# A one-core transformer layer whose opening is reordered: loads queued by need, stacks copied on chip

## The chip, the cores and the metric

The kernel runs on one core of a Trainium2 chip. The metric is the device time of one execution in microseconds; several runs are made and the median is taken. The core has five engines with a queue of instructions each: TensorE (PE, matmuls into PSUM), VectorE (DVE), ScalarE (ACT), GpSimd (POOL) and SyncE (SP, which here only issues transfers). They wait for each other through semaphores that are written out by hand.

## The reference

A pre-norm layer on x of shape (4, 256, 256): four batches of 256 rows of width 256. All of it is in float32.

```
h = layernorm(x)
q, k, v = h @ Wq.T, h @ Wk.T, h @ Wv.T
q, k = q*cos + rotate_half(q)*sin, k*cos + rotate_half(k)*sin     # over the whole width of 256
split into 16 heads of 16
mem_out = elu1(q) @ (elu1(k).T @ v) / (elu1(q) . sum elu1(k))     # elu1(t) = elu(t) + 1
attn = softmax(q @ k.T / 4) @ v
x = x + (sigmoid(gate)*mem_out + (1 - sigmoid(gate))*attn) @ Wo.T
h = layernorm(x)
x = x + fwht(silu(h @ W1.T) * (h @ W3.T)) @ W2.T                  # hidden width 1024
```

fwht is the normalised Walsh-Hadamard transform along the hidden axis. The kernel applies it to W2 instead of to the hidden values, once, at the start.

## The kernel before, in words

**Precision.** Each float32 operand of the projections is split into a high part (rounded by a ScalarE copy to float32r) and a low part (the rest, by a subtraction). A product is three matmuls: high by high, high by low, low by high.

**The stacks.** For the scores, the split sits in the contraction instead. `q_stack` and `k_stack` hold for each of 16 heads a column block of 256 and, on the partitions, three slots of 16 rows: q is (high, low, high), k is (high, high, low), so that one matmul sums the three products. Rows 48 to 63 are zero. Rows 64 and 65 are one in `k_stack`; in `q_stack` they are zero in the score pass and hold the negated row maximum (high, low) in the exp pass, so that the second product comes out shifted. `rotate_half` pairs column i with i + 128, so q and k are computed turned, with features on the partitions: a tile for the first 128 (c = 0) and one for the second (c = 1), and heads 0 to 7 lie in the first, 8 to 15 in the second. The rotated values (`roped`) are split into `part_hi` and `part_lo`, written to DRAM (`parts`, L261) and read back into the slots with the head moved from the partitions to the columns (`load_stacks`, L263 to L275), six copies of 128 KB for each half of the heads.

**The rounds.** The batches go through a pipeline of rounds, from -1 to 4. In round r the attention of batch r and the feed-forward part of batch r - 1 are computed, and q, k, v of batch r + 1 are prepared. A round has a score phase (`scores`, then the row maxima on VectorE, L628), the transpose of the maxima (L911), two small transfers of the negated maxima into row 64 and 65, and an exp phase (`shifted_scores` L919, exp on ScalarE L367, the product with v L936). The stacks of batch r + 1 are loaded in round r, half by half, as soon as the exp phase has read eight heads (L269). All of the order is written out by hand, engine by engine; each engine works through its list in order, and SP's list of transfers is one more such queue.

**The opening** (round -1). SP loads x0, Wq, Wk, x1, W1, W3; when the splits of Wq, Wk, Wv are done, W2 (it shares their buffer `narrow_raw`), then x2, x3, and four pieces of Wo. ACT's queue loads the gate, the constants and Wv. GpSimd zeroes both stacks (L490, L534), sets ones in rows 64 and 65 (L536), and subtracts for the low parts of W1 and W3 (L542). ScalarE splits Wq, Wk, Wv (L313), copies the turned rows (L319), and splits W1 and W3 (L411). VectorE does the layer norm of batch 0 (L592 to L611), the low parts of the weights (L762), the rotation (L639, L644), the low parts of q and k (L649), the negative part (L653) and the features (L660). TensorE: transpose, q and k, v, transpose of batch 1, `hadamard(0)`, features turned (L948), `hadamard(1)`, scores of heads 0 and 1, memory (L959). Then round 0 begins with the projections of batch 1 mixed into the score phase, and `hadamard(2)` and `hadamard(3)` at heads 6 and 7.

**W2.** Four hadamard products (L1046, 128 rows of the transform each) and three butterflies, the first on GpSimd, the others on VectorE (L233), all in place between `w2_raw` (the same memory as Wq, Wk, Wv raw) and `w2_b` (that of W3 raw). So W2 can be loaded only after the splits of Wq, Wk and Wv, and the first butterfly waits for the low part of W3 (L227).

## Time and profile before

| | us |
|---|---|
| median of 3 runs | 251.93 |
| lowest, highest | 249.94, 252.10 |
| profiled execution | 254.45 |
| its span, first to last instruction | 252.6 |
| TensorE matmuls busy | 200.2 (79%) |
| VectorE busy | 174.9 (69%) |
| ScalarE busy | 97.8 (39%) |
| GpSimd busy | 95.7 (38%) |

The span is that of the profiled execution; its own time is 1.85 us longer than the span. The mean granted clock of TensorE is 0.932 of full speed. In the first 50 us TensorE is idle for more than half of the time.

### The profile page before, as it was taken

The page shows a single profiled execution, that of the slowest core. Times are in us where ns is not written, and L with a number is a line of the kernel's source. Part 1 is how long each engine was busy: PE and PEld are TensorE (multiplying, and loading weights), DVE is VectorE, ACT ScalarE, POOL GpSimd, SP SyncE. Part 2 cuts the span into 40 slices and gives each one's busy share as a digit, 9 for nine tenths or more (in the row PEclk, how much of TensorE's full clock was granted, in tenths as well). Part 3 has the DMA queues.
Part 4 walks back from the last instruction along what each step waited for, and adds up shares of the span by engine and source line. Part 5 has one row for each costly group of instructions (what it writes and reads, how often), then busy time and mean ns, then how long its engine had stood idle before and what let it go on. Part 6 is the DMA issues. An engine that isn't in the chain of part 4 may idle for free.

```text
span 252.6 us, 4048 instructions
## 1 busy us (share of the span) xinstructions
PE 200.2 (79%) x1444; PEld 169.1 (67%) x1444; DVE 174.9 (69%) x341; ACT 97.8 (39%) x196; POOL 95.7 (38%) x73
## 2 busy tenths in 40 slices
PE   0064066886897949999999699999879999959894
PEld 0064055873544939997788599877769986748893
DVE  6966862498898597838879967448998562962442
ACT  2261131042884012368810325686021577312231
POOL 7919500069450738323610492152021215111332
PEclk9999655799997997999999899999999999997999
DMA  6919299313087103002790130066800100000101
GB/s 217 384 29 260 86 176 120 38 43 130 0 122 114 22 31 111 31 2 51 79 128 1 43 114 20 4 91 99 109 0 0 49 0 3 1 1 0 44 0 42
DMA packets 16940, 17.67 MB, mean 70 GB/s; under 512 B 1676, under 2 KB 16268, under 8 KB 16908
## 3 DMA queue, kind: packets, MB, share of 16 engines
q1 hardware_dynamic: 16168, 16.68, 31.9%
q10 hardware_dynamic: 752, 0.73, 0.9%
q8 instruction: 11, 0.18, 0.4%
q14 instruction: 9, 0.07, 0.1%
HBM read 11.93 MB, written 5.24 MB: 68 GB/s over the span
## 4 chain that ended last, share of the span: by engine, by line
PE 43%; issue 22%; DVE 17%; POOL 8%; DMA 6%; SPq 2%; ACT 2%; POOLq 0%; DVEq 0%; ACTq 0%
DVE rowmax_pad L628 5%; DMA k_stack<-parts 5%; PE score_bank L901 5%; PE score_bank L1010 4%; PE exp_bank L919 4%; DVE xn L611 4%; PE down_bank L1032 4%; POOL hid_lo L525 4%; PE exp_bank L1010 3%; PE misc_bank L848 2%; DVE prod L639 2%; PE pv_bank L936 2%; PE misc_bank L849 2%; PE misc_bank L850 2%; PE misc_bank L969 2%
## 5 line engine op out<-in xcount | busy, mean ns | idle before, releaser
L628 DVE TENSOR_REDUCE rowmax_pad<-score_bank 128x2 f32<-128x512 f32 x64 | 42.8, 685 | 17.8 <-PE score_bank L901 17.8
L525 POOL TENSOR_TENSOR hid_lo<-wide_raw,hid_hi 128x256 fp32r<-128x256 f32 x32 | 25.0, 782 | 70.6 <-ACT hid_hi L400 67.1
L367 ACT ACTIVATE prob<-exp_bank 128x512 f32<-128x512 f32 x64 | 37.8, 601 | 15.4 <-PE exp_bank L919 15.1
L901 PE MATMUL score_bank<-k_stack,q_stack 128*128 128x256 f32 x128 | 31.1, 337 | 14.7 <-DVE rowmax_pad L628 10.5
L901 PEld LDWEIGHTS score_bank<-k_stack,q_stack 128*128 128x128 f32 x128 | 21.8, 205 | 20.0 <-DVE rowmax_pad L628 10.8
L919 PE MATMUL exp_bank<-q_stack,k_stack 128*128 128x256 f32 x128 | 28.5, 306 | 2.5 <-DMA q_stack<-nmT_lo 1.4
L919 PEld LDWEIGHTS exp_bank<-q_stack,k_stack 128*128 128x128 f32 x128 | 19.2, 189 | 14.0 <-issue 8.2
L506 POOL TENSOR_TENSOR roped<-prod 128x512 f32<-128x512 f32 x6 | 7.6, 1271 | 44.0 <-DVE prod L639 44.0
L738 DVE SCALAR_TENSOR_TENSOR wide_raw<-wide_raw,score_bank 128x256 f32<-128x256 f32 x16 | 6.7, 418 | 23.3 <-ACT wide_raw L394 23.3
L861 PE MATMUL misc_bank<-cst,xn 128*128 128x128 f32 x16 | 3.4, 351 | 23.9 <-DVE xn L611 23.9
L1032 PE MATMUL down_bank<-w_hi,hid_hi 128*128 128x256 f32 x64 | 17.5, 296 | 1.4 <-ACT hid_hi L400 1.4
L861 PEld LDWEIGHTS misc_bank<-cst,xn 128*128 128x128 f32 x16 | 2.3, 178 | 24.1 <-issue 13.1
L988 PE MATMUL pv_bank<-wo,att 128*128 128x256 f32 x64 | 16.3, 382 | 1.7 <-DVE att L723 1.7
L611 DVE TENSOR_SCALAR xn<-xs,mv,rstd 128x256 f32<-128x256 f32 x16 | 12.3, 809 | 7.6 <-POOL rstd L499 7.3
L1010 PE MATMUL exp_bank<-h2T_hi,w_hi 128*128 128x256 f32 x64 | 17.4, 294 | 0.0
L1010 PE MATMUL exp_bank<-h2T_hi,w_lo 128*128 128x256 f32 x64 | 17.1, 288 | 0.0
L1010 PE MATMUL score_bank<-h2T_hi,w_hi 128*128 128x256 f32 x64 | 17.0, 289 | 0.0
L1032 PE MATMUL down_bank<-w_lo,hid_hi 128*128 128x256 f32 x64 | 16.5, 281 | 0.0
L1010 PE MATMUL score_bank<-h2T_hi,w_lo 128*128 128x256 f32 x64 | 16.4, 280 | 0.0
L379 ACT ACTIVATE xs<-pv_bank 128x512 f32<-128x512 f32 x4 | 2.4, 598 | 35.1 <-DVE stats L592 35.1
L325 ACT ACTIVATE part_hi<-roped 128x512 fp32r<-128x512 f32 x8 | 5.0, 630 | 27.8 <-POOL roped L506 20.3
L936 PE MATMUL pv_bank<-prob,v_strips 128*32 128x256 f32 x192 | 15.3, 391 | 0.1
(117 smaller groups left out, 547.4 us busy)
## 6 DMA issues: line engine op xcount, KB each, us to landing
q_stack<-parts SPq DMA_DIRECT2D x24, 128.0 KB
k_stack<-parts SPq DMA_DIRECT2D x24, 128.0 KB
parts<-part_hi SPq DMA_DIRECT2D x8, 256.0 KB, 2.2
parts<-part_lo SPq DMA_DIRECT2D x8, 256.0 KB, 2.4
xs<-in_x SPq DMA_DIRECT2D x4, 256.0 KB, 6.6
wide_raw<-in_w1T SPq DMA_DIRECT2D x1, 1024.0 KB, 8.2
wide_raw<-in_w3T SPq DMA_DIRECT2D x1, 1024.0 KB, 10.0
narrow_raw<-in_w2T SPq DMA_DIRECT2D x1, 1024.0 KB, 6.0
```

The lines of the kernel that those rows point to most:

```text
L367: act.activation(prob[:, h % 8], exp_bank[h % 2][:], ACT.Exp, scale=SCALE).then_inc(prob_s, 1)
L506: pool.tensor_tensor(roped[:, c], prod[:, 2 * c], prod[:, 2 * c + 1], (ALU.subtract, ALU.add)[c]).then_inc(rope_sum, 1)
L525: pool.tensor_tensor(hid_lo[:, n % 3, :], ffn_work[n % 3], hid_hi[:, n % 3, :].bitcast(F32), ALU.subtract).then_inc(hid_lo_s, 1)
L611: dve.tensor_scalar(xn[:, tt, :], xs[:, b, tt, :], mv[:, tt, 0:1], rstd[:, tt:tt + 1], ALU.subtract, ALU.mult).then_inc(ln_xn, 1)
L628: dve.tensor_reduce(rowmax[:, h, :], score_bank[h % 2][:], AX.X, ALU.max).then_inc(rowmax_s, 1)
L738: dve.scalar_tensor_tensor(out=work, in0=work, scalar=1.0, in1=chunk_bank(n)[:, 0, :], op0=ALU.add, op1=ALU.mult).then_inc(gated_s, 1)
L901: mm = pe.matmul(bank[:, tt, :], q_stack[:, h, tt * P:tt * P + P], k_stack[:, h, :], start=True, stop=True)
L919: mm = pe.matmul(bank[:, tt, :], k_stack[:, h, tt * P:tt * P + P], q_stack[:, h, :], start=True, stop=True)
L936: mm = pe.matmul(bank[STRIP * j:STRIP * j + STRIP, half, :], v_strips[b % 2][:, tt, h, :], prob[:, h % 8, tt, :], start=(tt == 0), stop=(t ...
L988: mm = pe.matmul(bank[:, tt, :], att[:, g, tt * P:tt * P + P], wo[:, g, :], start=False, stop=(g == NG - 1), skip_group_check=True)
L1010: pe.matmul(bank[:, m, :], w[:, m, k, cols], h2T_hi[:, k, :], start=(k == 0 and w is w13_hi), stop=False)
L1032: pe.matmul(bank[:, tt, :], hid_hi[:, n % 3, tt * P:tt * P + P], w[:, c, :], start=(c == 0 and tt == 0 and w is w2_hi), stop=False, skip_g ...
```

## The change

**SP's queue.** After x0, Wq, Wk, x1, W1 it issues three transfers that fill rows 48 to 65 of `q_stack` with zeros, rows 48 to 63 of `k_stack` with zeros and rows 64 and 65 of it with ones, from a small tile `fill` of two times 256 columns that GpSimd sets. Then come the twelve stack copies of batch 0 and only then W3, W2, x2, the four pieces of Wo, x3.

**The stacks.** The columns of Wq and Wk and the rows of the tables are put in another order outside of the timed kernel (`by_dim`), so that partition p of a part holds dimension p // 8 of head p % 8. A copy then goes from `part_hi` or `part_lo` on chip straight to a slot; `parts` in DRAM, its writes and its semaphores go. The four copies of the high part are issued when that is ready, the two of the low part when that is. Splits of a later batch wait for these copies (`stack_in`) instead of for the writes. The matmuls read rows 0 to 65 of the stacks instead of all 128.

**GpSimd.** The memsets of the stacks go. W1's low part comes in four pieces ahead of round 0, W3's in four pieces in round 0, between the low parts of batch 1 and the first butterfly.

**ScalarE.** It splits W1 after `exp_elu(0)` and W3 after the copy of the turned features, instead of both ahead of v. All four hadamard products are copied out in round 0, between the two high parts of batch 1.

**VectorE.** `low_hT(0)` comes after the low part of Wk instead of before it, `ln_normalise(1)` ahead of the rope products.

**TensorE.** All four hadamard products come in round 0's score phase, after heads 5, 6, 7 and 8.

```diff
-            for m, w in enumerate((w1T, w3T)):
-                sp.dma_start(wide_raw[:, m], w.rearrange("(c p) n -> p c n", p=P)).then_inc(w13_in[m], 16)
-            sp.wait_ge(wqkv_hi_s, 3)
...
+            sp.dma_start(wide_raw[:, 0], w1T.rearrange("(c p) n -> p c n", p=P)).then_inc(w13_in[0], 16)
+            sp.wait_ge(fill_set, 2)
+            for rows, value in ((q_stack[3 * HD:MAXROW + 2], 0), (k_stack[3 * HD:MAXROW], 0), (k_stack[MAXROW:MAXROW + 2], 1)):
+                n = rows.shape[0]
+                sp.dma_start(rows.bitcast(F32), fill[0:n, value, :].unsqueeze(1).broadcast_to([n, NH, S])).then_inc(stack_zero, 16)
+
+            def late_loads():
+                sp.dma_start(wide_raw[:, 1], w3T.rearrange("(c p) n -> p c n", p=P)).then_inc(w13_in[1], 16)
+                sp.wait_ge(wqkv_hi_s, 3)
+                sp.wait_ge(wqkv_lo_s, 3)
+                sp.dma_start(w2_raw, w2T.rearrange("(c p) n -> p c n", p=P)).then_inc(w2_in, 16)
+                sp.dma_start(xs[:, 2], xv(x, 2)).then_inc(x_in[2], 16)
+                sp.wait_ge(wo_zero, 1)
...
+                sp.dma_start(xs[:, 3], xv(x, 3)).then_inc(x_in[3], 16)
...
             def load_stacks(b, c):
-                sp.wait_ge(parts_out[c], 32 * (b + 1))
                 if b == 0:
-                    sp.wait_ge(stack_zero, 2)
+                    sp.wait_ge(stack_zero, 48)
                 else:
                     sp.wait_ge(exp_ps, NH * (b - 1) + HH * (c + 1))
                     sp.dma_start(q_stack[MAXROW:MAXROW + 2, HH * c:HH * c + HH, :].bitcast(F32),
-                                 k_stack[MAXROW + 2:MAXROW + 4, HH * c:HH * c + HH, :].bitcast(F32)).then_inc(stack_in[c], 16)
-                for m, stack, slots in ((0, q_stack, (0, 1, 0)), (1, k_stack, (0, 0, 1))):
-                    for s, half in enumerate(slots):
-                        sp.dma_start(stack[HD * s:HD * s + HD, HH * c:HH * c + HH, :].bitcast(F32),
-                                     parts[b, half, c, m].rearrange("(h d) n -> d h n", d=HD)).then_inc(stack_in[c], 16)
+                                 fill[0:2, 0, :].unsqueeze(1).broadcast_to([2, HH, S])).then_inc(stack_in[c], 16)
+                for src, ready, slots in ((part_hi, part_hi_s, ((0, 0), (0, 2), (1, 0), (1, 1))),
+                                          (part_lo, part_lo_s, ((0, 1), (1, 2)))):
+                    sp.wait_ge(ready, DC * b + c + 1)
+                    for m, s in slots:
+                        sp.dma_start((q_stack, k_stack)[m][HD * s:HD * s + HD, HH * c:HH * c + HH, :].bitcast(F32),
+                                     src[:, c, m, :].bitcast(F32)).then_inc(stack_in[c], 16)
...
             for r in ROUNDS:
-                if has(r + 1):
-                    for c in range(DC):
-                        write_parts(r + 1, c)
                 if has(r):
                     load_max(r)
                 if has(r + 1):
                     for c in range(DC):
                         load_stacks(r + 1, c)
+                if r < 0:
+                    late_loads()
...
             evac_hT(0)                              # ScalarE
-            for m in range(2):
-                split_wide(m)
...
                 if r == 0:
-                    evac_hadamard(2)
-                    evac_hadamard(3)
+                    for u in range(4):
+                        evac_hadamard(u)
...
                 if r < 0:
+                    evac_hT(1)
                     exp_elu(0)
-                    evac_hT(1)
-                    evac_hadamard(0)
+                    split_wide(0)
                     evac_kfT(0)
-                    evac_hadamard(1)
+                    split_wide(1)
...
-            pool.memset(q_stack[:].bitcast(F32), 0.0).then_inc(stack_zero, 1)
+            for k in range(2):
+                pool.memset(fill[:, k, :], float(k)).then_inc(fill_set, 1)
...
             ln_power(0)
-            pool.memset(k_stack[:].bitcast(F32), 0.0).then_inc(k_zero, 1)
-            pool.wait_ge(k_zero, 1)
-            pool.memset(k_stack[MAXROW:MAXROW + 2].bitcast(F32), 1.0).then_inc(stack_zero, 1)
-            pool.wait_ge(stack_zero, 2)
             ln_power(1)
             pool.memset(wo[:], 0.0).then_inc(wo_zero, 1)
-            for m, done in enumerate((w1_lo_s, w3_lo_s)):
+            def wide_low(m):
                 pool.wait_ge(w13_hi_s, m + 1)
-                pool.tensor_tensor(w13_lo[:, m], wide_raw[:, m], w13_hi[:, m].bitcast(F32), ALU.subtract).then_inc(done, 1)
+                for k in range(DC):
+                    for half in range(2):
+                        cols = slice(half * 512, half * 512 + 512)
+                        pool.tensor_tensor(w13_lo[:, m, k, cols], wide_raw[:, m, k, cols], w13_hi[:, m, k, cols].bitcast(F32),
+                                           ALU.subtract).then_inc((w1_lo_s, w3_lo_s)[m], 1)
+            wide_low(0)
...
                 if r == 0:
+                    wide_low(1)
                     butterfly(pool, 0)
...
-                if m == 0:                          # VectorE
+                if m == 1:
                     low_hT(0)
             ln_statistics(1)
+            ln_normalise(1)
             rope_product(0, 0)
...
-                        pe.wait_ge(stack_in[h // HH], 112 * b + 96)
+                        pe.wait_ge(stack_in[h // HH], stack_count(b))
...
-                        mm = pe.matmul(bank[:, tt, :], q_stack[:, h, tt * P:tt * P + P], k_stack[:, h, :],
+                        mm = pe.matmul(bank[:, tt, :], q_stack[0:MAXROW + 2, h, tt * P:tt * P + P], k_stack[0:MAXROW + 2, h, :],
...
             transpose_rows(1)
-            hadamard(0)
             transpose_features(0)
-            hadamard(1)
...
-                    if h in (6, 7) and r == 0:
-                        hadamard(h - 4)
+                    if h in (5, 6, 7, 8) and r == 0:
+                        hadamard(h - 5)
```

## Rows read from the trace of the kernel before

**Rows 1.** Chain of waits: start us, us, what.
```profile
35.13 6.43 DMA k_stack<-parts
72.04 5.64 DMA k_stack<-parts
```

**Rows 2.** Timeline, VectorE, opening: start, us, engine, line, operation, count [idle before <-releaser].
```profile
5.78 7.16 DVE L611 TENSOR_SCALAR xn<-xs,mv,rstd 128x256 f32<-128x256 f32 x2 [0.88 <-POOL rstd L499]
...
22.17 2.45 DVE L644 TENSOR_TENSOR roped<-prod 128x512 f32<-128x512 f32 x1
...
25.31 4.21 DVE L649 TENSOR_TENSOR part_lo<-roped,part_hi 128x512 fp32r<-128x512 f32 x1
...
31.55 0.69 DVE L649 TENSOR_TENSOR part_lo<-roped,part_hi 128x512 fp32r<-128x512 f32 x1 [0.70 <-ACT part_hi L325]
32.16 0.73 DVE L611 TENSOR_SCALAR xn<-xs,mv,rstd 128x256 f32<-128x256 f32 x2
...
34.61 1.22 DVE L660 SCALAR_TENSOR_TENSOR feat<-roped,prod 128x1024 f32<-128x1024 f32 x1 [1.12 <-ACT prod L338]
```

**Rows 3.** Timeline, GpSimd, opening.
```profile
5.68 3.51 POOL L534 MEMSET k_stack<- 128x4096 f32 x1
9.25 3.54 POOL L536 MEMSET k_stack<- 2x4096 f32 x1
...
19.50 9.48 POOL L542 TENSOR_TENSOR w_lo<-wide_raw,w_hi 128x2048 fp32r<-128x2048 f32 x2
```

**Rows 4.** Timeline, ScalarE, opening.
```profile
7.56 1.15 ACT L313 ACTIVATE wqkv_hi<-narrow_raw 128x512 fp32r<-128x512 f32 x2 [0.81 <-DMA narrow_raw<-in_wkT]
14.21 0.60 ACT L319 ACTIVATE hT_hi<-misc_bank 128x512 fp32r<-128x512 f32 x1 [5.50 <-PE misc_bank L861]
...
24.65 0.63 ACT L325 ACTIVATE part_hi<-roped 128x512 fp32r<-128x512 f32 x1 [1.92 <-DVE roped L644]
```

**Rows 5.** Timeline, SP's issues of transfers: the first of batch 0's and of batch 1's.
```profile
32.73 1.41 SPq L274 DMA_DIRECT2D q_stack<-parts  x3
...
69.75 1.30 SPq L274 DMA_DIRECT2D q_stack<-parts  x3
```

**Rows 6.** Windows: busy us (count) of PE, PEld, DVE, ACT, POOL; granted clock, transfer share, GB/s.
```profile
20.00:23.00 3.00, 2.10 (x18) 1.90 (x16) 2.12 (x3) 0.60 (x1) 3.00 (x1) 1.00 1.05 352
34.00:46.50 12.50, 9.46 (x35) 7.68 (x34) 4.05 (x9) 2.86 (x5) 0.00 (x0) 0.50 1.11 128
...
71.50:77.50 6.00, 3.90 (x34) 2.18 (x30) 5.79 (x9) 4.29 (x9) 3.27 (x1) 1.00 0.93 115
```

**Rows 7.** Timeline, TensorE, hadamard products and the score phase of round 0.
```profile
33.85 1.91 PE L1046 MATMUL exp_bank<-narrow_raw,cst 128*128 128x256 f32 x4
...
49.10 0.74 PE L901 MATMUL score_bank<-k_stack,q_stack 128*128 128x256 f32 x4
50.75 0.50 PE L901 MATMUL score_bank<-k_stack,q_stack 128*128 128x256 f32 x2 [0.91 <-DVE rowmax_pad L628]
51.09 1.02 PE L1046 MATMUL exp_bank<-narrow_raw,cst 128*128 128x256 f32 x4
...
60.09 0.33 PE L911 MATMUL pv_bank<-cst,rowmax_pad 128*128 128x128 f32 x1 [0.79 <-DVE rowmax_pad L628]
```

**Rows 8.** Timeline, GpSimd, round 0.
```profile
57.57 4.67 POOL L233 TENSOR_TENSOR wide_raw<-narrow_raw 128x1024 f32<-128x1024 f32 x2
62.21 2.77 POOL L517 TENSOR_SCALAR prod<-roped 128x1024 f32<-128x1024 f32 x1
```

**Rows 9.** Timeline, TensorE and VectorE, start of batch 1's scores.
```profile
77.73 0.85 PE L901 MATMUL score_bank<-k_stack,q_stack 128*128 128x256 f32 x4 [1.80 <-DMA k_stack<-parts]
...
85.57 0.69 DVE L628 TENSOR_REDUCE rowmax_pad<-score_bank 128x2 f32<-128x512 f32 x1 [2.87 <-PE score_bank L901]
```

**Rows 10.** Transfers: KB, us to landing of W1; of the on-chip 16 KB copies of maxima.
```profile
wide_raw<-in_w1T SPq DMA_DIRECT2D x1, 1024.0 KB, 8.2
...
DMA to landing us min/median/max: 2.1/2.3/2.5
```

More of the change, by code:

```diff
@@ L252, in _ @@
-            sp.wait_ge(wo_zero, 1)
-            for j in range(4):
-                sp.dma_start(wo[STRIP * j:STRIP * j + HD, :, :],
-                             woT.rearrange("(g j e) n -> j e g n", j=4, e=HD)[j]).then_inc(wo_in, 16)
-            def write_parts(b, c):
-                for half, (t, ready) in enumerate(((part_hi, part_hi_s), (part_lo, part_lo_s))):
-                    sp.wait_ge(ready, DC * b + c + 1)
-                    sp.dma_start(parts[b, half, c].rearrange("m p n -> p m n"), t[:, c].bitcast(F32)).then_inc(parts_out[c], 16)
+            sp.dma_start(wide_raw[:, 0], w1T.rearrange("(c p) n -> p c n", p=P)).then_inc(w13_in[0], 16)
@@ new lines, in _ @@
+            sp.wait_ge(fill_set, 2)
[9 more added lines that the diff above has]
+                sp.wait_ge(wo_zero, 1)
+                for j in range(4):
+                    sp.dma_start(wo[STRIP * j:STRIP * j + HD, :, :],
+                                 woT.rearrange("(g j e) n -> j e g n", j=4, e=HD)[j]).then_inc(wo_in, 16)
+                sp.dma_start(xs[:, 3], xv(x, 3)).then_inc(x_in[3], 16)
@@ L299, in _ @@
             sp.wait_ge(y_out, 16 * TT * NB)
-            for c in range(DC):
-                sp.wait_ge(parts_out[c], 32 * NB)
         @block.scalar
@@ L773, in _ @@
             first_low_part(1)
-            ln_normalise(1)
             first_negative_part()
```

36 lines of the change are left out of this document (18 added, 18 removed).

## The prediction

> **What bounds the kernel now.** I read the busy time by stage first, then the chain of waits, then the timeline of each engine over the opening (0 to 60 us) and over the change from round 0 to round 1. After about 80 us TensorE is busy nearly all the time and the change touches only the order of SP's transfers there; so what it can win or lose lies ahead of that. In the opening the chain goes through VectorE, then through a transfer: the first score matmul waits until the `k_stack` copies land at 41.56, and the same wait comes back, shorter, at 77.68 [rows 1].
>
> VectorE is slow there for a reason that its own rows don't give. The two normalise instructions take 7.16 us together, a rope sum 2.45 and a low part 4.21, where the same low part takes 0.69 later [rows 2]. Each long one ends just as a GpSimd instruction does: two memsets of `k_stack` run from 5.68 to 12.79, the split of W1 and W3 from 19.50 to 28.98 [rows 3]. So I read their length as a wait for GpSimd, not as work. Two normalises take 0.73 us in all where GpSimd is idle (32.16, one row of the same view).
>
> **Step 1, the memsets of the stacks go.** GpSimd keeps two fills of 256 columns (3.51 us x 256/4096 = 0.22 us each [rows 3]), done by 1.3 us, ahead of the first normalise. That one ends at 5.78 + 0.73 = 6.5 instead of 12.94. Next late is ScalarE: it splits Wk and Wv until 8.71 ahead of `evac_hT(0)` [rows 4], so hT_hi is ready at 8.75 + 0.60 = 9.35 instead of 14.81, hT_lo 0.69 later. Projections start **5.5 us earlier**; the 6.4 us of VectorE are not all had. `low_hT(0)` now stands behind the split of Wk, which ends at 8.9, so this costs nothing. `ln_normalise(1)` moves ahead of the rope products: x1 is in SBUF, it fits between 10.8 and 14.6 (GpSimd's memset of `wo`, 0.96 us, may hold it once), and the products can't start before 15.3. Free.
>
> **Step 2, W1's and W3's splits leave the rope chain.** ScalarE splits W1 only after `exp_elu(0)`, so GpSimd has nothing to subtract while VectorE makes sums and parts: 2.45 - 0.69 and 4.21 - 0.69 [rows 2], together **5.3 us**. The first high part, ready at 25.28 [rows 4], comes at 25.28 - 5.5 - 1.8 = 18.0, the last low part at 32.24 - 10.8 = 21.4.
>
> **Step 3, no trip through DRAM.** Before, the first of six stack copies is issued at 32.73, behind four writes and their landing; it is now issued at 18.0. In round 1 the six land 7.9 us after the first issue (69.75 to 77.68), in round 0 8.8 us [rows 1, 5]. Both are bounds from neighbours; an on-chip copy of 128 KB is nowhere in the trace. What limits a copy? While stacks are loaded the transfer engines are busy all the time at 115 to 128 GB/s, where the loads of W2 and x to 128 partitions ran at 352 GB/s [rows 6]. The rows are 1 KB in both cases and the source is DRAM in both; what differs is 16 target partitions. So I take the target as the limit and the copy as costing the same: 12.4 us for twelve (34.0 to 46.4; 128 GB/s over 34.0 to 46.5 [rows 6]), 1.03 us each. The six land at 18.0 + 7.9 = 25.9. Meanwhile the features come: they ended 3.6 us after the last low part (35.83 against 32.24 [rows 2]), 0.6 of it the normalise that is now earlier, so at 24.4; their transposes take 1.1, and TensorE is ready at 25.5. First score matmul at **26.0 instead of 41.60: -15.6 us**. The three fills of fixed rows are 36 rows of 16 KB, 0.58 MB, behind W1 on SP's queue: at 115 GB/s 5.1 us after W1 (issued at 2.74, landed 8.2 us later [rows 10]), done by 16 to 17, so just covered. If W1 or they were 2 us later, every 1 us would be paid.
>
> The skill has a rule on each side here. The Trainium skill, "SBUF — State Buffer", section on the DMA port swizzle: 16 neighbouring partitions reach 4 of 16 ports, about 109 GB/s; by that a copy is 1.2 us and the sum stays as it is. The Trainium skill, "DMA: Bandwidth & Descriptors", section "Why small descriptors are slow (HBM only)", says that transfers within SBUF don't pay the small-packet penalty; by that alone the copies would be quicker, which is the second case below.
>
> **Step 4, what is moved behind the copies.** SP now issues W3 (1 MB) only after all twelve stack copies, then W2 (1 MB), x2, four pieces of Wo, x3. Wo, x2 and x3 are wanted later than 60 us, and the issues are over 30 us ahead of `load_max(0)`: free. W3 and W2 are not. Of the 7.9 us above, 7.9 - 6 x 1.03 = 1.7 are start and landing; I put 1.2 ahead and 0.5 behind. The copies' data runs from 18.0 + 1.2 = 19.2 to 31.7; 2 x 1.05 MB at 352 GB/s are 5.9 us; with 0.6 us to land and rounding, W2 is there at **38.2**. TensorE reaches head 5 with scores 4 and 5 ended at 49.84 [rows 7] - 15.6 = 34.2 and stands at `hadamard(0)` for 4.0 us; heads 6 to 15, and by them VectorE's maxima, are behind it. A hadamard product took 1.91 us at 1.2 GHz and 1.02 us at 2.4 GHz [rows 7]; I take 1.7, so head 6 goes at 39.9, where it went at 50.75: 10.8 us gained are left. From head 6 to the transpose of the maxima it took 9.34 us [rows 7]; one more hadamard product is in it (0.7). The pause costs clock: the granted clock was 0.50 from 34.0 to 46.5 [rows 6], so until 5 us after the scores had begun; what is 2 us of matmuls at 2.4 GHz is 4 us at 1.2 GHz, and I count half of that extra as hidden by VectorE's maxima (1.0). VectorE, which lagged by 1.1 us at head 6, starts without a backlog: together +0.6. The transpose comes at 49.8 instead of 60.09: **-10.2 us**.
>
> **Step 5, GpSimd later in round 0.** W3's low part (9.48/2 = 4.74 us [rows 3]; four pieces, so that VectorE waits for a piece of 1.2 us at most) now stands ahead of the 4.67 us butterfly and the 2.77 us negative part [rows 8]. VectorE's second butterfly, the next normalise, `exp_elu(1)` on ScalarE and the weights stand behind these. The last hadamard product ends at about 43.8 (39.9, four heads at 0.35, three products at 0.85), ScalarE's copy and high part at 45.0, the low part at 46.3, the butterfly at 46.3 + 4.74 + 4.67 = 55.7: 5.9 us after the transpose of the maxima, where it was 2.15 us (62.24 against 60.09), so 3.8 us later. Lowest cost 0, highest 4.7. It is taken up by TensorE's 1.80 us of idle time before the scores of batch 1 and VectorE's 2.87 us before the third maximum of round 1 [rows 9]; nearest to those rows I take **+1.2 us**. W1's low part runs from 25.1 to 29.9, beside VectorE work that reads at most one operand in SBUF; rope sums come after it anyway.
>
> **Step 6, the rest.** Score matmuls with 66 instead of 128 rows have the same 256 columns: 0. Lower bound none, upper bound small, since PE rows here differ by columns only. Rounds 1 to 3 lose the writes of parts, but their stack copies start at the eighth exp head as before: 0, hidden behind TensorE's work. The column order of Wq, Wk and the tables is data: 0.
>
> **Sum:** -10.2 + 1.2 = -9.0 us. Against the profiled execution (254.45 us, span 252.6) that gives 245.4. It lay 2.5 us above the median; the runs shown spread over 2.2 us. From the median of 251.93 it is **242.9 us**.
>
> **The rivals.**
> - *On-chip copies are quick* (at the 352 GB/s of the wide loads [rows 6]). For: the trace can't tell a slow target from a slow DRAM pattern for certain. Then issues (0.46 us each) set the pace, twelve are issued by 23.6, W2 lands by 31, the hadamard products wait for nothing. TensorE waits for features: -16.0 + 0.7 for two more products, + 2 for GpSimd, which is then later against the rest: -13.3, **238.6 us**.
> - *GpSimd's lag is paid in full*: normalise 2 and `exp_elu(1)` hold up the exp phase, and the stack copies of the second half with it. -10.2 + 4.7 = -5.5, **246.4 us**. Against: the idle times above.
> - *Copies somewhat slower* (1.6 to 2.0 us each): W2 lands at 45 to 50, the gain is eaten at `hadamard(0)`: within 1%, about **251 us**.
> - *Slower than before*: the place is `hadamard(0)` at head 5. An on-chip copy of 16 KB took 2.3 us to land [rows 10]; if reading and writing SBUF at once made each of the twelve cost that, data ends at 19.2 + 27.6 = 46.8, W2 lands at 53.3, the transpose comes at 53.3 + 1.7 + 9.9 = 64.9, +4.8 + 1.2: **257.9 us**. It decides from about 1.85 us per copy (no change) and 2.1 us (1% slower). Against: 2.3 us is latency for the most part, and six DRAM copies in a row didn't pay it each.
> - *A slow clock behind the pause* (inside the forecast's range): the granted clock was 0.50 from 34.0 to 46.5 [rows 6], with the pause before 41.6 in it. The Trainium skill, "TensorE: Matmul & The Clock Gate", section "HAM oscillation", says that pauses between matmuls bring the clock down to half. By that rule the sum changes only if heads beyond those counted run at 1.2 GHz: all of heads 6 to 15 at that level would take some 3 us more of matmul time (14 us at 0.50 do what 7 do at 1.00), of which VectorE's 0.6 us per maximum hides most, and the result would be 244.
>
> **Chances.** Forecast 0.50 (its own range 241 to 246), quick copies 0.20, GpSimd in full 0.13, slower copies 0.09, slower than before 0.08. The range goes from 238 to 249: it holds the first three cases and leaves out the last two. Within 1% (249.4 to 254.4) is what a measurement of this kernel can't tell from no change. Faster 0.83, same 0.09, slower 0.08.
>
> **What would show it.** Step 1: normalises of 0.73 us in all, projections at 10.1. Step 2: no rope sum or low part over 0.8 us. Step 3: first score matmul at 26.0 and not a wait for features; if 25.5 or earlier, copies are quick. Step 4: an idle stretch of about 4 us on TensorE ended by the load of W2. Step 5: butterfly on GpSimd ends 6 us after the transpose of the maxima (2.2 before) and the first score of batch 1 comes 17.6 to 19 us after it. The forecast is wrong if copies within SBUF cost something other than those from DRAM, or the fills are not done by 19.

## The result

The changed kernel is slower: a median of 257.80 us (257.42 to 258.36, 4 runs) against 252.01 us before, ratio 1.0249 with a 95% interval of 1.019 to 1.0308. Run again later beside other kernels it gave 258.73 us, ratio 1.0201 (1.0149 to 1.0253). Of each kernel some runs come out some per cent slower at a lower clock: medians take all runs, ratios and their 95% intervals leave those out. The forecast was 242.9 us and a range of 238 to 249; the time is that of the rival that I gave 8 chances in 100, 257.9 us, though only part of its mechanism is what happened.

The opening did get shorter; it is given back, and more. VectorE's timeline of the changed kernel (columns as in [rows 2]):

```profile
16.62 0.69 DVE L647 TENSOR_TENSOR roped<-prod 128x512 f32<-128x512 f32 x1
...
18.01 0.69 DVE L652 TENSOR_TENSOR part_lo<-roped,part_hi 128x512 fp32r<-128x512 f32 x1
...
20.72 0.69 DVE L652 TENSOR_TENSOR part_lo<-roped,part_hi 128x512 fp32r<-128x512 f32 x1 [0.69 <-ACT part_hi L325]
```

No instruction is long any more; the last low part ends at 21.41 (before 32.24, [rows 2]). Then SP's issues, and TensorE from the first score on:

```profile
3.33 1.02 SPq L251 DMA_DIRECT2D q_stack<-fill  x1
4.41 1.45 SPq L251 DMA_DIRECT2D k_stack<-fill  x2
20.20 1.26 SPq L277 DMA_DIRECT2D q_stack<-part_hi  x2
...
28.00 0.60 SPq L254 DMA_DIRECT2D wide_raw<-in_w3T  x1
28.70 0.44 SPq L257 DMA_DIRECT2D narrow_raw<-in_w2T  x1
29.18 3.56 SPq L258 DMA_DIRECT2D xs<-in_x  x1
32.78 5.68 SPq L261 DMA_DIRECT2D wo<-in_woT  x4
```

```profile
29.79 1.22 PE L904 MATMUL score_bank<-k_stack,q_stack 66*128 66x256 f32 x4 [3.60 <-DMA k_stack<-part_lo]
...
45.15 2.07 PE L1049 MATMUL exp_bank<-narrow_raw,cst 128*128 128x256 f32 x4 [7.62 <-DMA narrow_raw<-in_w2T]
...
56.51 0.33 PE L914 MATMUL pv_bank<-cst,rowmax_pad 128*128 128x128 f32 x1 [0.78 <-DVE rowmax_pad L631]
...
78.83 1.20 PE L904 MATMUL score_bank<-k_stack,q_stack 66*128 66x256 f32 x4
```

The first score comes 11.8 us earlier than before, the first hadamard product of the score phase stands still for 7.62 us until W2 lands, the transpose of the maxima comes 3.6 us earlier (60.09, [rows 7]), and the first score of batch 1 already 1.1 us later (77.73, [rows 9]). That last row carries no wait: TensorE was busy for 17.48 of the 18.84 us of its exp phase, at about half clock. The windows of the changed kernel show the transfers and this phase (columns as in [rows 6]): the copies, W3 and W2 at full rate, W2's tail, and the exp phase of round 0.

```profile
21.30:36.30 15.00, 7.59 (x40) 7.22 (x41) 6.29 (x13) 3.45 (x3) 4.92 (x4) 0.56 1.12 116
36.30:42.50 6.20, 1.23 (x10) 0.97 (x8) 3.75 (x6) 2.43 (x2) 1.27 (x1) 0.91 1.05 365
42.50:45.10 2.60, 0.00 (x0) 0.00 (x0) 0.00 (x0) 0.00 (x0) 0.00 (x0) 0.50 1.16 153
...
59.99:78.83 18.84, 17.48 (x88) 9.84 (x89) 14.37 (x18) 10.82 (x19) 10.37 (x5) 0.55 0.38 44
```

And that of the kernel before in the same phase, from its first exp score to the first score of batch 1:

```profile
63.57:77.73 14.16, 11.15 (x88) 6.39 (x89) 13.04 (x18) 11.41 (x21) 5.73 (x3) 1.00 0.45 67
```

### The profile page after: what moved, and what is told of

Same layout as the page of the kernel before. It is cut to its first block, busy times and chain, and to the rows that moved or that the text cites. A ratio compares the mean times of both kernels' runs of the same rounds, so it can differ in the third digit from the quotient of the medians.

```text
span 256.6 us, 4033 instructions
## 1 busy us (share of the span) xinstructions
PE 205.2 (80%) x1444; PEld 171.8 (67%) x1444; DVE 165.1 (64%) x341; ACT 98.2 (38%) x196; POOL 86.2 (34%) x78
## 4 chain that ended last, share of the span: by engine, by line
PE 36%; issue 20%; DMA 15%; POOL 12%; DVE 8%; SPq 6%; ACT 1%; POOLq 0%; DVEq 0%; ACTq 0%
DMA narrow_raw<-in_w2T 6%; DMA k_stack<-fill 6%; SPq L277 4%; PE score_bank L1013 4%; POOL hid_lo L524 4%; PE score_bank L904 4%; PE exp_bank L922 4%; DVE rowmax_pad L631 3%; PE exp_bank L1013 3%; PE down_bank L1035 3%; PE pv_bank L939 2%; DMA k_stack<-part_lo 2%; PE misc_bank L972 2%; PE exp_bank L1049 2%; POOL w_lo L541 2%
## 5 line engine op out<-in xcount | busy, mean ns | idle before, releaser
L631 DVE TENSOR_REDUCE rowmax_pad<-score_bank 128x2 f32<-128x512 f32 x64 | 42.9, 685 | 27.5 <-PE score_bank L904 27.2
L904 PE MATMUL score_bank<-k_stack,q_stack 66*128 66x256 f32 x128 | 32.0, 343 | 14.5 <-DVE rowmax_pad L631 9.0
L904 PEld LDWEIGHTS score_bank<-k_stack,q_stack 66*128 66x128 f32 x128 | 22.3, 208 | 19.2 <-DVE rowmax_pad L631 8.7
L922 PE MATMUL exp_bank<-q_stack,k_stack 66*128 66x256 f32 x128 | 31.7, 339 | 2.2 <-DMA q_stack<-nmT_lo 1.4
L922 PEld LDWEIGHTS exp_bank<-q_stack,k_stack 66*128 66x128 f32 x128 | 21.7, 213 | 16.0 <-issue 8.2
L1035 PE MATMUL down_bank<-w_hi,hid_hi 128*128 128x256 f32 x64 | 17.5, 296 | 1.4 <-ACT hid_hi L400 1.4
L939 PE MATMUL pv_bank<-prob,v_strips 128*32 128x256 f32 x192 | 18.0, 452 | 0.0
L498 POOL TENSOR_TENSOR rstd<-var_eps,mhalf 128x2 f32<-128x2 f32 x8 | 6.0, 751 | 29.0 <-DVE var_eps L604 28.8
L400 ACT ACTIVATE hid_hi<-wide_raw 128x256 fp32r<-128x256 f32 x32 | 13.3, 416 | 4.1 <-DVE wide_raw L744 3.8
L394 ACT ACTIVATE wide_raw<-exp_bank 128x256 f32<-128x256 f32 x16 | 6.2, 385 | 22.5 <-PE exp_bank L1017 20.5
L530 POOL TENSOR_TENSOR wide_raw<-wide_raw,narrow_raw 128x1024 f32<-128x1024 f32 x4 | 11.3, 2828 | 7.9 <-DVE narrow_raw L714 7.9
## 6 DMA issues: line engine op xcount, KB each, us to landing
xs<-in_x SPq DMA_DIRECT2D x4, 256.0 KB, 7.6
wide_raw<-in_w1T SPq DMA_DIRECT2D x1, 1024.0 KB, 12.2
```

The lines of the kernel that those rows point to most:

```text
L400: act.activation(hid_hi[:, n % 3, :], ffn_work[n % 3], ACT.Copy).then_inc(hid_hi_s, 1)
L530: pool.tensor_tensor(v, v, rden, ALU.mult).then_inc(norm_lin, 1)
L631: dve.tensor_reduce(rowmax[:, h, :], score_bank[h % 2][:], AX.X, ALU.max).then_inc(rowmax_s, 1)
L904: mm = pe.matmul(bank[:, tt, :], q_stack[0:MAXROW + 2, h, tt * P:tt * P + P], k_stack[0:MAXROW + 2, h, :], start=True, stop=True)
L922: mm = pe.matmul(bank[:, tt, :], k_stack[0:MAXROW + 2, h, tt * P:tt * P + P], q_stack[0:MAXROW + 2, h, :], start=True, stop=True)
L939: mm = pe.matmul(bank[STRIP * j:STRIP * j + STRIP, half, :], v_strips[b % 2][:, tt, h, :], prob[:, h % 8, tt, :], start=(tt == 0), stop=(t ...
```

## The experiments

Fifteen runs were made, of thirteen kernels: e15 repeats e1, and e14 is the changed kernel again. Those with a ratio are compared with the kernel before on the same chip. The table gives the stages of each profile in us, so that each theory can be read at its own place: first score, first hadamard product of the score phase, transpose of the maxima of round 0, first score of batch 1, transpose of the maxima of round 1, the length of the exp phases of rounds 1 and 2 (first exp score to first score of the next batch), the granted clock of the exp phase of round 0, the span, and the median of the runs. The stages are those of one profiled execution each, and that isn't always a typical one: it lay 2.4 us above the median in the kernel before and 2.7 us above it in e8. So a difference of 1 or 2 us between two rows is read with the medians beside it.

| kernel | score 0 | hadamard | maxima 0 | score 1 | maxima 1 | exp 1 | exp 2 | clock exp 0 | span | median |
|---|---|---|---|---|---|---|---|---|---|---|
| before | 41.6 | 51.1 | 60.1 | 77.7 | 105.0 | 16.25 | 15.82 | 1.00 | 252.6 | 252.0 |
| changed | 29.8 | 45.2 | 56.5 | 78.8 | 107.7 | 17.05 | 17.16 | 0.55 | 256.6 | 257.8 |
| e1 before, 66 rows | 41.7 | 50.9 | 59.9 | 80.7 | 109.8 | 16.30 | 15.86 | 0.60 | 258.0 | 259.3 |
| e15 the same again | 41.6 | 51.0 | 60.0 | 81.8 | 110.5 | 16.30 | 15.94 | 0.50 | 256.0 | 257.6 |
| e2 fills first | 31.1 | 45.0 | 57.6 | 79.8 | 107.8 | 16.98 | 17.32 | 0.58 | 255.9 | 258.5 |
| e3 W3, W2 first | 43.2 | 51.1 | 64.7 | 87.0 | 115.5 | 16.99 | 17.23 | 0.50 | 264.2 | 264.7 |
| e4 Wo late | 28.4 | 42.2 | 54.6 | 76.8 | 104.5 | 16.97 | 17.32 | 0.57 | 252.7 | 256.3 |
| e5 memsets, 66 | 26.9 | 42.3 | 54.7 | 77.0 | 104.8 | 17.01 | 17.33 | 0.57 | 252.9 | 255.5 |
| e6 memsets, 128 | 28.5 | 44.2 | 55.5 | 76.5 | 103.8 | 17.03 | 17.32 | 0.71 | 252.5 | 255.1 |
| e7 low part early | 27.5 | 41.3 | 52.9 | 74.0 | 101.7 | 16.91 | 17.29 | 0.81 | 250.2 | 252.2 |
| e8 hadamard late | 27.3 | 41.5 | 50.6 | 73.3 | 101.9 | 17.05 | 17.26 | 0.79 | 250.1 | 249.2 |
| e10 reset whole | 27.1 | 41.1 | 50.4 | 71.1 | 98.7 | 16.96 | 17.32 | 0.92 | 246.6 | 249.9 |
| e9 no clash | 31.1 | 39.5 | 48.5 | 66.9 | 93.0 | 16.25 | 15.87 | 1.00 | 240.4 | 241.95 |
| e11 mixed | 27.9 | 35.4 | 44.4 | 64.3 | 90.6 | 16.25 | 16.25 | 0.79 | 238.4 | 240.2 |
| e12 mixed, 66 | 28.1 | 35.3 | 44.3 | 65.9 | 94.8 | 16.30 | 16.11 | 0.53 | 243.5 | 245.2 |
| e13 all on chip | 27.4 | 35.7 | 44.7 | 66.6 | 94.5 | 17.03 | 17.16 | 0.85 | 242.7 | 243.0 |

**Rows: 66 against 128.** The edit, the same for the exp scores:

```diff
-mm = pe.matmul(bank[:, tt, :], q_stack[:, h, tt * P:tt * P + P], k_stack[:, h, :],
+mm = pe.matmul(bank[:, tt, :], q_stack[0:MAXROW + 2, h, tt * P:tt * P + P], k_stack[0:MAXROW + 2, h, :],
```

> The kernel before with one thing of the change: score matmuls of both phases read rows 0 to 65 of the stacks instead of all 128 (the rest is zero rows, so the values are the same). Theory ROWS: the granted clock of TensorE falls where these matmuls are most of its work, because fewer rows are driven. Then the exp phase of round 0 (60.1 to 77.7 before, granted 1.00) shows about 0.6 as in the changed kernel, takes 2 us or more longer, and the run is 2 to 5 us above the kernel before. Rival PAUSE: the clock falls only because the changed kernel stands idle from 37.5 to 45 and its windows lie otherwise. Then this kernel keeps 1.00 there and gives the time before, 252 within 1 us.

Measured: the runs spread from 254.75 to 261.62 us, too wide for a ratio; the times up to the maxima were those of before, the exp phase took 17.35 us instead of 14.16. So it went in again with five rounds.

> The kernel e1_before_66_rows again, with five rounds: the kernel before with 66 rows in the score matmuls. Theory ROWS: 4 to 6 us above the kernel before, about 257, as e12_mixed_66 stands to e11_mixed, with the exp phase of round 0 below a granted clock of 0.7. Rival: it is a matter of how the pauses fall, and the fastest run of e1, 254.75, is the usual one: 1 to 2 us above the kernel before.

Measured: 257.60 us (256.29 to 260.64), ratio 1.0183 (1.0156 to 1.021). Its exp phase of round 0, which took 14.16 us at 1.00 before:

```profile
63.43:81.81 18.38, 17.66 (x88) 10.57 (x89) 12.96 (x18) 10.98 (x20) 5.72 (x3) 0.50 0.34 45
```

And on another kernel, e11 below:

> The kernel e11_mixed with 66 rows in the score matmuls instead of 128, the same edit as in e1_before_66_rows on another kernel. Theory ROWS: granted clock in the exp phase of round 0 falls below 0.7, that phase is 2.5 us longer or more, and the run is 3 to 6 us slower than e11_mixed. Rival: without a pause before it the clock holds and the time is the same within 1 us.

Measured: 245.17 us (244.27 to 245.43) against 240.18 (238.73 to 241.08), 5.0 us; their ratios to the kernel before, 0.9723 (0.9672 to 0.9774) and 0.953 (0.9485 to 0.9574), don't overlap. The exp phase of round 0 in e11 and in e12:

```profile
47.89:64.26 16.37, 13.51 (x88) 8.07 (x88) 12.83 (x18) 11.49 (x21) 5.69 (x3) 0.79 0.46 78
```

```profile
47.78:65.87 18.09, 17.20 (x88) 10.18 (x89) 12.89 (x18) 10.76 (x19) 5.74 (x3) 0.53 0.40 70
```

The reader is to see the same 88 matmuls, that begin at the same time behind the same work, take 17.20 instead of 13.51 us at a lower granted clock. The phase itself is 1.7 us longer, and most of the rest is lost in the score phase behind it (28.97 instead of 26.36 us, clock 0.82 against 0.94). 66 rows cost about 5 us, shown in two kernels. In a third pair, e5 and e6, they cost far less: 0.4 us between the medians, 1.2 us of span from the transpose of the maxima of round 0 to the end, and the two ratios, 1.0186 (1.0094 to 1.0278) and 1.0144 (1.0053 to 1.0236), aren't told apart. The clock of the 128-row kernel was at 0.71 there already, and it waited for its copies; that the price depends on what clock is left to lose is my reading of the three pairs and isn't shown. Of the kernels here this pair is the nearest to the changed one.

**Fills, and the order of the loads.** e2 moves the three fills ahead of W1, e3 issues W3 and W2 behind the fills and ahead of the stack copies:

```diff
 sp.dma_start(xs[:, 1], xv(x, 1)).then_inc(x_in[1], 16)
-sp.dma_start(wide_raw[:, 0], w1T...)      # e2: behind the fills
 sp.wait_ge(fill_set, 2)
 (the three fills)
+sp.dma_start(wide_raw[:, 0], w1T...)      # e2
+sp.dma_start(wide_raw[:, 1], w3T...)      # e3, instead of in late_loads
+sp.dma_start(w2_raw, w2T...)              # e3, instead of in late_loads
```

> The changed kernel with its three fills of fixed stack rows issued ahead of W1 instead of behind it. In the changed kernel they land at 20.2 and the first stack copy, ready at 18.0, waits for them. Theory FILLS: the first copy is issued at 18.0, everything behind it (W3, W2, the hadamard product at head 5) comes about 2.2 us earlier, the run is about 2 us faster than the changed kernel, near 255.5. Rival: the fills delay W1, whose split is wanted at 23; or what the opening gains is given back in the exp phase at a lower clock, and the time stays near 257.8.

> The changed kernel with W3 and W2 issued behind the fills and ahead of the stack copies of batch 0, so that nothing that the hadamard products need stands behind the copies. Theory QUEUE: TensorE no longer waits 7.6 us at the first hadamard product; first score matmul 29.8 plus at most 3 us for the loads that now go first; the transpose of the maxima comes at 49 to 51 instead of 56.5; the run gives 250 to 253, 5 to 7 us below the changed kernel. Rival ROWS: the transpose comes as early as that, but the exp phase runs at half clock and GpSimd's work (W3's low part ahead of the butterfly) stands in the way of it, so that only 2 to 3 us are left, near 255.

Both fell. e2: 258.46 us (255.47 to 261.27), ratio 1.0154 (1.0075 to 1.0234), first copy issued at 19.82, where the changed kernel had it at 20.20 and, run again (e14), at 19.79: the place ahead of W1 doesn't help the fills. e3 was the worst of all, 264.70 us (259.05 to 266.03, too wide for a ratio). The hadamard products no longer waited for W2, but the scores did for the copies. From 10 to 20 us fills and W3 went together at 119 GB/s; W3, issued at 5.99, took 20.9 us to land, W2, issued at 10.73, took 26.6 us, the first copy was issued at 22.85, and TensorE stood for 16.9 us until the copies of the first half landed at 43.2. The expectation had allowed at most 3 us for the two loads. Without fills (e13 below) the same two loads took 10.1 and 6.7 us.

> The changed kernel with the four pieces of Wo and x3 issued after the maxima of batch 0 instead of right behind x2. Nothing wants them before 80 us. Theory TAIL: W2's last bytes share the transfer engines with the Wo pieces, which go to 16 partitions each; W2's data should have been there at 42.5 and landed at 45.15. Then W2 lands at about 43 and the run is 2 us faster than the changed kernel, about 255.8. Rival: W2's landing is set by its own bytes and the copies ahead of it; landing and time stay at 45.1 and 257.8.

The edit moves four Wo transfers and x3 behind `load_max(0)`. Measured: 256.30 us (254.41 to 258.32, 8 runs), ratio 1.0093 (1.0053 to 1.0133). W2 landed 13.8 us after the first score instead of 15.4: 1.5 us of the tail were Wo's, and TAIL holds.

```diff
-three fills from the tile fill
+pool.memset(q_stack[:].bitcast(F32), 0.0)           # at 0.7
+pool.memset(k_stack[:].bitcast(F32), 0.0)           # after the normalise of batch 1
+pool.memset(k_stack[MAXROW:MAXROW + 2].bitcast(F32), 1.0)
```

> The changed kernel without its three fill transfers: GpSimd sets the fixed rows by memsets as before, but in its idle time (q_stack at 0.7, k_stack after the normalise of batch 1, at 14.4 to 21.4). Matmuls still read 66 rows. Theory FILLS: the first stack copy is issued at 18.0 and not at 20.2, W1 lands earlier too, the hadamard product at head 5 runs 2 to 3 us earlier; the run is 1 to 3 us faster than the changed kernel, about 255 to 256, with the exp phase of round 0 still at half clock. Rival: the memsets hold VectorE or the copies up and nothing is won.

> The kernel e5_memsets_66 with the score matmuls of both phases on all 128 rows (rows 66 to 127 are zeros). Theory ROWS: the granted clock of the exp phase of round 0 goes back to 1.00 and stays higher later (mean above 0.92 against 0.885), the exp phase is 2 us or more shorter, and the run is 4 to 6 us faster than e5_memsets_66, about 250. Rival PAUSE: the stop at the first hadamard product alone sets the clock; then both give the same time within 1 us.

Measured: 255.46 us (254.27 to 256.41) and 255.08 us (253.58 to 257.76). In e5 the first copy was issued at 17.25 and W2 landed 2.9 us earlier than in the changed kernel, as theory FILLS has it; in e6, whose opening differs in nothing from e5's, the high part was ready later, the copy was issued at 18.70, and W2 landed 1.0 us earlier. The ratio of e5 can't be told from that of the changed kernel run again, 1.0201. So the trace shows that the wait for the fills goes, but not what that is worth at the end. ROWS, which forecast 4 to 6 us, did not hold in this pair, as told.

**GpSimd and the hadamard products.** e7 is e6 with Wo late and this on GpSimd; e8 also moves the products:

```diff
 rope_sums(r + 1, 0)
+if r == 0:
+    wide_low(1)             # e7: was ahead of butterfly(pool, 0)
-if h in (5, 6, 7, 8) and r == 0:
-    hadamard(h - 5)
+if h in (10, 11, 12, 13) and r == 0:   # e8
+    hadamard(h - 10)
```

> The kernel e6_memsets_128, with Wo and x3 issued after the maxima of batch 0 (as in e4_wo_late) and with W3's low part on GpSimd between the two rope sums of batch 1, where GpSimd stands idle from 40.4 to 49.1 in the changed kernel, instead of ahead of the butterfly. Theory GPSIMD: butterfly, negative part and normalise of round 0 end some 4.9 us earlier against the transpose of the maxima, the stop of TensorE ahead of head 6's exp goes; with W2 landing 2 to 3 us earlier the run is 3 to 5 us faster than e6_memsets_128, about 246. Rival: those waits are covered by idle time anyway (I had priced them at 1.2) and only W2's 2 us are won.

> The kernel e7_low_early with the four hadamard products after heads 10 to 13 instead of 5 to 8, and their copies on ScalarE behind the copy of v. Theory QUEUE: TensorE works through heads 5 to 10 while W2 is still on its way; the stop of about 6 us at head 5 shrinks to 1 us or none, the transpose of the maxima comes 4 to 5 us earlier and the run is 3 to 5 us faster than e7_low_early, about 242. Rival: the butterflies, now later against the maxima, take it back on VectorE and GpSimd in the exp phase, and 0 to 2 us are won.

Measured: 252.22 us (ratio 1.002, 0.9973 to 1.0067) and 249.17 us (0.9894, 0.9842 to 0.9946). In e7 GpSimd's negative part ended 4.4 us after the transpose of the maxima, in the changed kernel 9.5 us; the exp phase of round 0 took 17.64 us against 17.52 in e6. All of the gain lies ahead of the maxima, where W2 came sooner. With the lag gone the copies were the bound (e7, TensorE):

```profile
74.00 0.74 PE L913 MATMUL score_bank<-k_stack,q_stack 128*128 128x256 f32 x4 [2.98 <-DMA k_stack<-part_lo]
```

So the theory GPSIMD fell, its rival stands. e8 won 2.3 us at the maxima; its median is 3.0 us below that of e7, at the low end of what QUEUE forecast. Its profiled execution keeps only 0.7 us at the first score of batch 1, where TensorE waits 4.80 us for the copies, but that execution lay 2.7 us above the median; e10 below, with the same order, still has 2.9 us there.

**The opening alone.** e9 is the kernel before with steps 1 and 2 and nothing on chip; W3 is issued as before, at 3.4 us, W2 behind the splits as before, which is now 10.8 instead of 16.8 us, and the first two hadamard products run before the scores. Besides, x2 is issued behind the copies of batch 0, Wo and x3 behind the maxima of batch 0.

```diff
 ln_power(0)                               # GpSimd
-(memsets of k_stack)
 ln_power(1)
+pool.wait_ge(ln_xn, 2 * TT)
+(memsets of k_stack)
-for m in range(2):                        # ScalarE, behind evac_hT(0)
-    split_wide(m)
+evac_hT(1); exp_elu(0); split_wide(0); evac_hadamard(0); evac_kfT(0); evac_hadamard(1); split_wide(1)
```

> The kernel before with only steps 1 and 2 of my prediction: GpSimd's memset of k_stack after the normalise of batch 1, the splits of W1 and W3 and their low parts after exp_elu(0), the normalise of batch 1 ahead of the rope products; Wo and x3 issued after the maxima of batch 0. The trip of the parts through DRAM, the early loads of W3 and W2, the hadamard products in the opening and 128 rows stay. Theory CLASH: VectorE's waits for GpSimd (6.4 and 5.3 us) were the loss of the opening and these two steps win 10.8 us alone: first score matmul at 30.8, transpose of the maxima at 49.3, no stop for W2; with 1 us for GpSimd and clock the run gives 243. Rival: the pause and the clock eat most of it, 247 to 250, as in the kernels so far, where 3 to 9 us of a shorter opening left 0 to 3 us at the end.

Measured: **241.95 us** (240.07 to 243.47), ratio 0.96 (0.9541 to 0.9658). Maxima at 48.5, 11.6 us earlier than before, and the gain stays to the end (12.2 us of span, 10.5 us of median). The first stack copy is issued 10.8 us earlier than before (21.91 against 32.73), which is the sum of steps 1 and 2, so the gain is there ahead of the place to which Wo and x3 were moved. What that move adds wasn't tried by itself in this kernel. The exp phase keeps its clock:

```profile
52.09:66.92 14.83, 11.19 (x90) 6.42 (x89) 13.25 (x18) 11.91 (x22) 5.64 (x3) 1.00 0.57 94
```

The rival, that pauses and clock eat a shorter opening, fell with it: what ate it in the other kernels is W2 behind the copies, the copies of later batches, and the 66 rows. The price of each is in the pairs. e11 adds the on-chip copies to e9 for batch 0 alone (`if b == 0` in `load_stacks`, the column order of Wq and Wk turned by dimension; the parts of later batches still go through DRAM).

> The kernel e9_before_no_clash with the on-chip copies for batch 0 alone; later batches go through DRAM as before, 128 rows, W3 and W2 loaded ahead of the copies. Theory COPY: without fills and without loads behind them the first copy goes at 18.0 and the first score matmul comes at 27, 3 to 4 us ahead of e9_before_no_clash; the run is 2 to 4 us faster than it, about 240. Rival: W2's load is still in the queue when the copies are issued and holds them up, so that nothing is won against e9_before_no_clash.

Measured: **240.18 us** (238.73 to 241.08), ratio 0.953 (0.9485 to 0.9574), the fastest of all. First score 3.2 us ahead of e9 and 2.0 us of span kept; the two intervals of the ratios overlap a little, so the last 1.8 us are likely and not certain.

**On-chip copies in later batches.** e10 is e8 with the reset of rows 64 and 65 from `k_stack[MAXROW + 2:MAXROW + 4]`; e13 is e11 with all batches on chip.

> The kernel e8_hadamard_late with one thing put back: rows 64 and 65 of q_stack are reset ahead of each half's copies from two rows of zeros of k_stack, 8 KB in one piece each, as before the change, instead of from one row of 1 KB repeated eight times. In the changed kernel the reset moves 16 to 33 GB/s for 1.5 us, before it took an eighth of a microsecond. Theory RESET: the copies of a later batch land 1.5 us sooner, the exp phases of rounds 1 and 2 shrink from 17.05 and 17.3 to 16.3 and 15.8 us as before, the run is 2 to 3 us faster than e8_hadamard_late, about 246.5. Rival ISSUE: it is the copies from the chip (issued at 0.6 us each against 0.43, 103 GB/s against 115 to 128) that are slower, and the exp phases stay above 16.8.

> The kernel e11_mixed with the copies of the later batches on chip too, instead of through DRAM (the reset of rows 64 and 65 from zero rows of k_stack as before). Theory COPIES: copies from the chip land later after their first issue than those from DRAM (9.3 to 9.9 us against 8.2), and since they are issued only after the eighth exp head, the scores of the next batch wait: exp phases of rounds 1 and 2 of 17.0 and 17.3 us instead of 16.25 and 16.25, the run 1.5 to 2.5 us slower than e11_mixed, about 242. Rival: the writes of the parts that go away free the transfer engines and SP's queue, and the time is the same or better.

Measured: e10 249.88 us, exp phases 16.96 and 17.32: RESET fell. e13 243.03 us (241.11 to 244.49), ratio 0.9624 (0.9587 to 0.9661) against e11's 0.953 (0.9485 to 0.9574), exp phases 17.03 and 17.16: COPIES holds, about 2.8 us between the medians. In round 0 too: there the exp phase takes 18.40 instead of 16.37 us, and TensorE waits 4.67 instead of 1.69 us for the copies. SP's rows of batch 2 in e13, then in e11:

```profile
106.36 0.65 SPq L272 DMA_DIRECT2D q_stack<-k_stack  x1
107.06 1.22 SPq L278 DMA_DIRECT2D q_stack<-part_hi  x2
```

```profile
102.52 0.62 SPq L280 DMA_DIRECT2D q_stack<-k_stack  x1
103.18 1.33 SPq L284 DMA_DIRECT2D q_stack<-parts  x3
```

Three issues in 1.33 us through DRAM, two in 1.22 us on chip; e13's TensorE then waits 0.58 us for `k_stack<-part_lo` at 116.24, 9.2 us after the first copy's issue. Whether the issue or the transfer weighs more isn't separated.

**W3 and W2 behind the copies.** e10 and e13 both have all copies on chip, 128 rows, no fills, and Wo and x3 late. They differ in the order of the change itself: e10 issues W3 and W2 behind the twelve copies and has its hadamard products at heads 10 to 13, with W3's low part in pieces in round 0; e13 loads both first, as before, with two products ahead of the scores. SP's rows in e13:

```profile
3.51 0.48 SPq L247 DMA_DIRECT2D wide_raw<-in_w3T  x1
10.80 0.37 SPq L250 DMA_DIRECT2D narrow_raw<-in_w2T  x1
17.53 1.32 SPq L278 DMA_DIRECT2D q_stack<-part_hi  x2
```

The two loads hold nothing up: first copy at 17.53 (e10: 17.41), first score at 27.4 (e10: 27.1). The transpose of the maxima comes 5.7 us earlier, and the medians are 243.03 and 249.88 us, the ratios 0.9624 (0.9587 to 0.9661) and 0.9884 (0.9842 to 0.9926). So without fills the new order of the queue, with what it moves on the other engines, bought no time at the scores and cost nearly 7 us, the largest price of any pair here.

> The changed kernel, unchanged, on the chip of this call, so that its distance to the kernel before is taken beside that of the others. All theories expect 256.5 to 258.5, 1.5 to 3% above the kernel before.

Measured: 258.73 us, ratio 1.0201 (1.0149 to 1.0253).

## Why the prediction was wrong, step by step

**Steps 1 and 2 were right.** Projections at 10.6 (forecast 10.1), rope products at 15.3 (15.3), last low part at 21.4 (21.4). With nothing else of the change (e9; Wo, x2 and x3 moved besides) they give 241.95 us, 10.5 us below the kernel before, where they were worth 10.8 us in the sum.

**Step 3 was mis-sized in two terms.** The fills were to be "just covered": they landed at 20.2 instead of 16 to 17, and the first copy, whose high part was ready at 17.98, waited 2.2 us for them. I had costed 0.58 MB at the rate of the stack loads; from 15 to 19.5 us it ran at 29 GB/s, with the transfer engines busy for a third of the time (share 0.31). W1, which shared the engines with the fills, took 12.2 us to land instead of 8.2. And the six copies landed 9.6 us after the first issue, not 7.9. The twelve took 15.0 us (21.3 to 36.3, the window above), 1.25 us each and not 1.03. First score 29.8 instead of 26.0.

Here I had the better number at hand and did not use it: the Trainium skill, "SBUF — State Buffer", section on the DMA port swizzle, gives about 109 GB/s for 16 partitions, by which I estimated 1.2 us per copy. The trace agrees with the page: 1.25 us, 105 GB/s. I noted that with it "the sum stays as it is". It doesn't: twelve copies stand ahead of W2, and 0.2 us of each are 2 us. The other rule that I weighed, of the Trainium skill, "DMA: Bandwidth & Descriptors", section "Why small descriptors are slow (HBM only)", is that transfers within SBUF escape the penalty of small packets. Whether they do, no run here shows. What I drew from it, copies at 352 GB/s, every run with such copies contradicts: into 16 partitions they took 1.25 us each, longer than the 1.03 us from DRAM.

**Step 4 had the right place and the wrong time.** W2 landed at 45.15, not 38.2: 2.2 us of fills, 2.5 us of slower copies, and 2.3 us of a tail in which Wo's pieces, which I had called free, shared the engines (e4: 1.5 us of it). From its landing to the transpose of the maxima it took 11.4 us, where the working said 11.6. The stop was 7.6 us instead of 4.0. The step also took for granted that W3 and W2 must go behind the copies for these to come early; e13 against e10 shows that they need not, once the fills are gone, and that this order, with the hadamard products and splits it moves, costs nearly 7 us. I had put this mechanism down as the case "slower" and asked 2.1 us per copy for it (the sums of that rival give 1.8 us for no change and 2.0 for 1%, not 1.85 and 2.1); W2 came 7 us late at 1.25 us per copy, since three terms erred in the same direction. In the changed kernel it left the transpose of the maxima 3.6 us ahead. The 6.7 us by which it came later than forecast are the largest part of the 13 us below.

**Step 5 was right about GpSimd and wrong about what follows.** GpSimd was late as worked out (negative part at 9.5 us after the maxima; the working gave 8.7). But the first score of batch 1 came 22.3 us after the maxima, where the sign was 17.6 to 19. That isn't GpSimd's doing as far as the runs show: in e7, without its lag, the exp phase is no shorter than in e6 (17.64 against 17.52), TensorE waiting for the copies there; in the changed kernel TensorE is busy nearly all of it, at 0.55.

**Step 6 failed: two terms put at 0 weren't.** "Score matmuls with 66 instead of 128 rows have the same 256 columns: 0." The columns, and the time of one matmul at a given clock, are the same. The clock isn't. e15 prices it at 1.8% (1.6 to 2.1) of the kernel before, e12 at 5.0 us of e11. I had even named the granted clock as a risk, but had tied it to the pause alone (and priced all of heads 6 to 15 at half clock at 3 us, where my own bracket, 14 us for 7, makes it 7). Also in step 6 I wrote 0 for the later stack copies, "hidden behind TensorE's work": the exp phases of rounds 1 and 2 grew by 0.8 and 1.3 us, as in each kernel with those copies; without them they grew by nothing in round 1 and at most 0.4 in round 2 (e9, e11, e12). e13 against e11 prices these copies at 2.8 us, that of batch 1 included.

Which term made the sign isn't shown. No run takes the 66 rows alone out of the changed kernel. The nearest, e6, has 128 rows and no fills and is still slower than before, ratio 1.0144 (1.0053 to 1.0236); with Wo and W3's low part moved as well (e7) it is level, 1.002 (0.9973 to 1.0067). By the pairs, W2's place in the queue, the later copies and the rows each have their part in it.

In the profiled execution the forecast's span was 243.6 and the changed kernel's 256.6. The 13 us: 6.7 at the transpose of the maxima of round 0 (steps 3 and 4), 3.5 from there to the first score of batch 1 (clock, copies), 1.6 to the maxima of round 1 (clock 0.82 against 0.88), 2.1 in the two exp phases, less 1.0 in round 2, where the changed kernel's clock was 1.00 against 0.94. Between the medians the forecast is off by 14.9 us and not by 13: the profiled execution of the kernel before lay 2.4 us above its median, that of the changed kernel 0.6. Where those last 2 us are isn't known.

## What to carry to other kernels

When transfers are put in order of need, cost the queue to its end: each one that goes first is paid by the last that is waited for, at the rate of its own target partitions, and a small error per transfer counts once for each. Before that, look whether the queue is empty when the urgent transfer becomes ready: here W3 and W2 could land by 17.5 us, and without the fills putting them behind the copies won nothing. Take the clock as a resource: an edit that leaves a matmul's columns alone but drives fewer rows need not be free; the granted clock of the stage shows it. And try the parts of a change one by one: two of this one's (the memset's place, the split's place, with Wo and x2, x3 moved) were worth 10 us, and the rest cost 16.

## What the runs showed of the hardware that I had not expected

- Score matmuls on 66 rows, with 62 rows of zeros left out, came with a lower granted clock: 0.53 against 0.79 (e12, e11), and 0.50 against 1.00 (e15, before), in the exp phase of round 0 behind the same work. In the exp phases of rounds 1 and 2, with 145 to 151 matmuls in some 16 us instead of 88, the clock stayed at 1.00 with either. The single matmul has the same length at the same level: four score matmuls in a row take 1.22 us at half clock and 0.74 at full clock with 66 rows as with 128.
- A VectorE normalise that met a GpSimd memset waited to the end of it: two took 7.16 us before, 0.73 us in the changed kernel. A rope sum and a low part beside a GpSimd subtraction took 2.45 and 4.21 us, 0.69 each without it. Not every pair clashes: in e9 rope products, rope sums and low parts ran beside the memsets of `k_stack` (13.37 to 20.45) at 0.69 us or less each.
- A transfer from one row of 1 KB to 2 rows of eight such (16 KB) ran at 16 to 33 GB/s; from rows that lie whole it took an eighth of a microsecond. The time of the kernel did not change with it (e8 and e10, ratios 0.9894 and 0.9884).
- SP takes 0.6 us to issue a copy of 128 KB from a part on chip, 0.43 to 0.47 us from DRAM.
- The fills of fixed rows from one row of 1 KB slowed the loads beside them: W1 took 12.2 us to land in the changed kernel, 7.7 to 8.3 us without fills (before, e9, e10, e13).
